# All of a round's expert parts behind the attention values, where one stood between scores and values

## Time and profile before

| | |
|---|---|
| median of 3 runs | 738.81 us (736.51 to 739.65) |
| profiled execution | 737.3 us, of which the span of the trace is 734.6 us |
| PE matmul busy | 617.4 us, 84% of the span |
| ACT busy | 566.3 us, 77% |
| DVE busy | 418.1 us, 57% |
| POOL busy | 160.2 us, 22% |
| granted PE clock, mean | 0.953 |
| sigmoids, line 662 | 512 instructions, 1068 and 1069 ns each |
| wait of ACT ahead of them for the scores | 25.1 us for `S` in 42 places, 12.0 us for `UO` in 21 |

### The profile page before, as it was taken

How to read it: one execution, slowest core, us unless ns; L and a number is a source line. 1 busy time by engine, 2 the same in 40 slices (tenths; PEclk the granted TensorE clock), 3 DMA queues, 4 the chain that set the end, 5 groups by cost and what they waited for, 6 DMA issues and landing times. The chain is left out here.

```text
span 734.6 us, 15277 instructions
## 1 busy us (share of the span) xinstructions
PE 617.4 (84%) x5928; PEld 255.2 (35%) x5928; DVE 418.1 (57%) x1107; ACT 566.3 (77%) x661; POOL 160.2 (22%) x149
## 2 busy tenths in 40 slices
PE   3587999999999999999999999999999999217840
PEld 2452211112223444442234444422344444107730
DVE  6875185910654555526765555367655553687953
ACT  1579899998999888889998888899988888004520
POOL 1122000000041222240412222314122223143442
PEclk9999999999999999999999999999999999758985
DMA  8600001610035444210364442103634421039921
GB/s 323 226 29 30 29 9 53 267 65 9 1 116 190 127 140 141 81 55 12 119 201 125 144 141 80 45 21 115 195 111 153 140 73 44 15 115 303 296 91 36
DMA packets 47639, 82.02 MB, mean 112 GB/s; under 512 B 5456, under 2 KB 25168, under 8 KB 47568
## 3 DMA queue, kind: packets, MB, share of 16 engines
q1 hardware_dynamic: 45088, 76.31, 32.1%
q0 software_dynamic: 2048, 4.20, 1.9%
q10 hardware_dynamic: 432, 0.54, 0.3%
HBM read 64.59 MB, written 16.45 MB: 110 GB/s over the span
## 5 line engine op out<-in xcount | busy, mean ns | idle before, releaser
L662 ACT ACTIVATE res<-S 128x1024 f32<-128x1024 f32 x348 | 349.3, 1068 | 27.5 <-PE S L772 14.1
L786 PE MATMUL AV<-res,vg 128*8 128x512 f32 x2048 | 310.4, 596 | 2.4 <-DVE coll L1160 2.4
L662 ACT ACTIVATE res<-UO 128x1024 f32<-128x1024 f32 x164 | 175.3, 1069 | 11.6 <-PE S L772 11.0
L584 POOL TENSOR_TENSOR work<-work 128x512 f32<-128x512 f32 x64 | 81.6, 1275 | 262.6 <-DVE work L1281 262.5
L772 PE MATMUL S<-qT,kT 32*128 32x512 f16 x696 | 103.4, 386 | 2.3 <-ACT res L662 2.0
L859 PE MATMUL GB<-xT,gu_ring 128*128 128x128 f16 x1164 | 81.8, 220 | 12.3 <-DVE work L1281 4.7
L636 ACT ACTIVATE work<-work,scl 128x512 f32<-128x512 f32 x64 | 46.6, 728 | 50.7 <-DVE work L1274 50.7
L859 PEld LDWEIGHTS GB<-xT,gu_ring 128*128 128x128 f16 x1164 | 65.5, 98 | 46.1 <-DVE work L1281 15.0
L556 POOL DMA_INDIRECT xs_dram<-xrow,slot x32 | 31.2, 974 | 211.2 <-DVE slot L1261 202.7
L1274 DVE TENSOR_SCALAR work<-GB,scl 128x512 f32<-128x512 f32 x56 | 45.3, 809 | 55.5 <-PE GB L859 55.5
L772 PEld LDWEIGHTS S<-qT,kT 32*128 32x128 f16 x696 | 25.7, 91 | 132.8 <-ACT res L662 79.0
(11 more groups left out here) (230 smaller groups left out, 635.7 us busy)
## 6 DMA issues: line engine op xcount, KB each, us to landing
gu_ring<-gu_dram SPq DMA_DIRECT2D x60, 512.0 KB, 3.8
dn_ring<-dn_dram SPq DMA_DIRECT2D x60, 256.0 KB, 3.3
work<-in_gu SPq DMA_DIRECT2D x8, 512.0 KB, 10.7
gu_dram<-gu_ring SPq DMA_DIRECT2D x8, 512.0 KB, 2.6
ys_dram<-work SPq DMA_DIRECT2D x60, 64.0 KB, 2.6
work<-in_down SPq DMA_DIRECT2D x8, 256.0 KB, 11.2
dn_dram<-dn_ring SPq DMA_DIRECT2D x8, 256.0 KB, 2.9
work<-xs_dram SPq DMA_DIRECT2D x4, 448.0 KB, 4.8
```

The source lines that it names most:

```text
L584: nc.gpsimd.tensor_tensor(hid[u % 2], prod[u % 2], sg[u % 2], ALU.mult).then_inc(hid_ready, 1)
L662: nc.scalar.activation(res[:, k % 2, 2 * half:2 * half + 2, :].rearrange("p h t -> p (h t)"), score_banks(i, k, half).rearrange("p h t -> ...
L786: mm = nc.tensor.matmul(AV[32 * j:32 * j + HD, :], vg[:, s, G * g + j, :], res[:, k % 2, j, :], start=s == 0, stop=s == ST - 1)
```

## The change

Only the order of PE's instructions in the rounds changes. Before, the first part of a round stood between scores(k) and values(k−1), and a second part behind the values. After, all parts of the round stand behind the values, one right after the other. The same instructions are issued, with the same semaphores; the order on ACT, DVE, POOL and SP stays as it was. `hidden_out` in rounds 58 to 60 and `project_first` keep their places.

```diff
--- before.py
+++ after.py
@@ -955,8 +955,6 @@
                             readers = [(slot_ready, i)]
                         if LAST_UNIT < k <= LAST_UNIT + LAG:
                             readers = hidden_out(i, NU - LAG + k - LAST_UNIT - 1, readers)
-                    for u, part in parts[:1]:
-                        readers = unit_part(i, u, part, readers)
                     if PROJECT_ROUND <= k < PROJECT_ROUND + NG - 1:
 
                         project_first(i, k - PROJECT_ROUND, readers)
@@ -964,9 +962,7 @@
                         values(i, k - 1)
                     elif i > 0:
                         values(i - 1, ROUNDS - 1)
-                    if (LAG, 1) in parts[:1]:
-                        readers = shared_out(i, readers)
-                    for u, part in parts[1:]:
+                    for u, part in parts:
                         readers = unit_part(i, u, part, readers)
                         if (u, part) == (LAG, 1):
                             readers = shared_out(i, readers)
```

## The result

The changed kernel takes 786.46 us (median of 4 runs, 783.74 to 787.96) against 738.0 us: a ratio of 1.0654, 95% interval 1.0633 to 1.0675. That is 48.5 us slower; forecast were 785.0 and, against the 738.8 known then, 46.2.

What follows compares the result with a forecast made beforehand. PE was taken to set the pace in rounds 22 to 57. Terms of 4.3, 7.1, 3.0 and 1.4 gave 15.8 us per block, 47.4 for three, less 1.2: 46.2 above 738.8, so 785.0 (chance 0.76), range 768 to 801.

Steps and rivals of the forecast that it cites:

- The bank's waits, +4.3: PE's waits for `GB` per block: 10.5 us come with back-to-back parts, 6.2 go, net 4.3 more.
- The silu, +7.1: Values wait for ACT's sigmoids queued behind a gate's silu, in rounds after certain gates; 7.1 us more per block.
- The collapse, +3.0: First values of a group wait for DVE's collapse: 1.74 more in round 33, 1.25 in round 49, per block.
- Rounds 14 to 21, +1.4: Where ACT sets the pace: shared gate of round 14 later, 1.1; transposes behind late values in round 21, 0.3; per block.
- Round 22 of blocks 2 and 3, −1.2: The gate's wait of about 0.6 us for DVE's tile copy is covered behind the values; 1.2 us less.
- Rounds 36 to 47: A walk through these rounds with all forecast waits in order: 34.9 us where the trace has 30.0.
- The clock: Rival, chance 0.07: granted clock falls in the stretch as in 60 to 80 us; 28 us more, 813.
- the clock there is below 1.00: Sign that the forecast's sum is wrong: granted clock below 1.00 in rounds 22 to 57.
- only the bank's waits count: Rival, chance 0.10: silu and collapse sink into ACT's idle 12 of 90 us; 15.9 us more, 755.
- ACT sets the pace: Rival, chance 0.03: ACT sets the pace throughout, so PE's waits come and go unseen; 739.
- faster: Rival, chance 0.04: PE's new waits hide behind ACT's work, only the gain of 19.8 us is left; 719.

Runs made afterwards that it cites:

- pairs back: The changed order, but in rounds with two parts the first part stands between scores and values again; 770.71 us, ratio 1.0446.
- singles back: The kernel before, but in the nine rounds with two parts both stand behind the values; 763.7 us, ratio 1.0351.
- silu later: The changed kernel, but on ACT each silu stands one round later, behind the next round's sigmoids; 769.22 us, ratio 1.0423.
- collapse first: The changed kernel, but on DVE the collapse of rounds 32 and 48 stands in front of that round's expert parts; 778.79 us, ratio 1.0551.
- both: The changed kernel with each silu one round later on ACT and the collapse of rounds 32 and 48 first on DVE; 758.11 us, ratio 1.0287.
- gate and turn pairs: The kernel before with another table of rounds: each of nine pairs holds a gate before the values and a turn behind; 731.44 us, ratio 0.9907.

## Why the prediction was right, point by point

The numbers are from the distances of the scores' starts, round by round, in the timelines of both kernels; block 3, where the clock stayed at 1.00. The mechanisms came out as forecast, term by term; what the sum lacked is 3.0 us for the clock and 0.2 per block in round 22.

- *The bank's waits, +4.3.* Measured +4.3 (rounds 22 to 58 with the silu and collapse rounds taken out). Singly: a gate in front of a turn 0.97, an up in front of a gate 0.91, a turn in front of an up 0.71; the pace from start to start plus the reader's time was enough, though no such pair was in the old trace. The kernel with only the pairs back (770.7) and the one with only the singles back (763.7) show both halves apart.
- *The silu, +7.1.* Measured +7.0: 1.02 in rounds 38, 40, 45 and 52, 1.13 in round 57, 1.35 in round 26, 0.46 in round 28. (The prediction names the values by their data: values 37 run in round 38.) Its second sigmoid "at 269.69 + 0.90" is a slip, since that sigmoid starts at 269.69; the end at 270.72 and the 4.3 us from the gate are right. The later silu shows that it is the silu's place. What the working did not see is the smaller part, the silu's own 0.61 on ACT where values stand right behind scores; in the changed kernel the latency covers it, so the sum was not off.
- *The collapse, +3.0.* Measured 1.75 in round 33 and 1.25 in round 49, and the collapse in front of the other work took both away.
- *Rounds 14 to 21, +1.4.* Measured 1.10 in rounds 14 and 15 and 0.33 in round 21, and nothing in either with the singles back, whose order there is the old one. Another 0.2 in round 22, again values right behind scores, was not in the sum.
- *Round 22 of blocks 2 and 3, −1.2.* Measured −0.6 in each.
- *Rounds 36 to 47* take 34.95 us (269.24 to 304.19) in block 1 of the changed kernel; 34.9 had been worked out.

That gives 15.4 in block 3 and, without the clock, 15.4 in block 2 and 16.0 in block 1: 46.7, where 46.2 had been worked out.

*The clock* was the rival with 0.07, and a little of it came true, at another price than stated. By the prediction's own sign ("the clock there is below 1.00") the sum is wrong here: it put the clock at nothing, and in blocks 1 and 2 the clock is 0.98. PE in rounds 33 and 34 of block 1 of the changed kernel:

```profile
257.59 0.39 PE L772 MATMUL S<-qT,kT 32*128 32x512 f16 x2
259.95 1.50 PE L786 MATMUL AV<-res,vg 128*8 128x512 f32 x8 [1.98 <-DVE coll L1156]
261.39 1.46 PE L859 MATMUL GB<-xT,gu_ring 128*128 128x128 f16 x12
```

And the windows of rounds 33 and 34 in blocks 1 and 3, and of two microseconds behind the wait in block 1:

```profile
257.58:267.16 9.58, 6.70 (x65) 3.11 (x64) 3.73 (x7) 4.78 (x6) 1.28 (x1) 0.82 0.36 104
...
586.45:594.53 8.08, 5.20 (x66) 2.58 (x66) 3.73 (x7) 4.78 (x6) 1.28 (x1) 1.00 0.35 106
...
261.00:263.00 2.00, 2.00 (x20) 1.31 (x16) 0.11 (x1) 0.00 (x0) 0.00 (x0) 0.50 0.04 15
```

An up that takes 0.84 elsewhere takes 1.46 here: behind the 1.98 us wait for the collapse the clock was at 1.2 GHz (0.50) for a while, which cost 1.50 us in block 1 and 1.46 in block 2. So 3.0 us of the profiled execution are the clock. That brings the worked-out 46.2 to 49.2, where the profiled executions differ by 786.63 − 737.3 = 49.3. That both agree to 0.1 is in part luck, for the rounds of the three blocks differ by 49.7. And the forecast of 785.0 lies within 1.5 of the median in part because the 738.8 it started from was 0.8 above the kernel before as timed now. The clock did not fall all over the stretch, as the rival had it; one place did it, the one where this change makes PE wait longest.

The rival by which only the bank's waits count (755) falls by the silu and collapse experiments, which bring back 17 and 8 us; the rivals "ACT sets the pace" and "faster" fall by the result.

## What to carry to other kernels

When an engine's order is rewritten, count for every moved instruction who reads its result and what is queued behind that reader: here the moved gate cost more through ACT's next sigmoids (7.0 us per block) than the parts cost through the bank that they share (4.3 net), and the collapse, which nobody moved, cost 3.0 because its cover was moved away. Independent work between two users of one buffer is worth at most the time until its reader is done (0.91 us behind a gate whose clip takes 0.81); where there isn't enough for all pairs, let the part with the shortest reader stand uncovered, which gained 0.9% without a new buffer. A matmul group whose first half is issued hides its wait in its busy time, so look for values of 1.6 us among values of 1.04, not only for brackets.

## What the runs showed of the hardware

The granted clock was not lost to many short waits here: with nine or more waits of 0.3 to 0.91 us in each stretch it stayed at 1.00 wherever no wait was longer (kernel before, singles back, collapse first, both, gate and turn pairs: 15 stretches). With a single wait of about 2 us in round 33 it fell in 4 of the 9 profiled places (the changed kernel, pairs back, silu later), each time for 1.2 to 1.6 us of cost. In each of the four it fell between 0.2 us before that wait's end and 1.1 us behind it, and not at the wait of 1.18 in round 49 of the same kernels. What decides between the 4 and the 5 stays open. The rule of the Trainium skill weighed ahead (TensorE: Matmul & The Clock Gate, A second HAM failure mode: psum-queue depth-cycling), by which brief idling between groups of matmuls makes the clock go to and fro, is not borne out by these waits, which were all for one bank, while the kernel that the Trainium skill tells of cycled through several. The clock fell at the one long wait.
